# A graph layer and a mixture of experts on one core: masks of the adjacency two pairs sooner in the row products, gathers ahead of additions, seven of eight additions in the neighbour sums

## What is computed

```python
h = layernorm(x)
mask = (adj > 0)                                  # 4096 x 4096, int32 in
agg = mask @ h / max(mask.sum(1), 1)
comb = concat([h @ W_self + b_self, agg @ W_nb + b_nb])
x1 = x + relu(comb @ W_comb + b_comb)
g = layernorm(x1)
score, idx = top_k(g @ Wg + bg, 2)
y = sum over the two experts of softmax(score) * (gelu(g @ W1[e] + b1[e]) @ W2[e] + b2[e])
return x1 + y
```

## Time and profile before

| | us |
|---|---|
| median of 3 runs | 512.1 |
| lowest, highest | 511.46, 516.15 |
| the profiled execution | 515.1 |
| its span, first to last instruction | 513.3 |

### The profile page before, as it was taken

How to read it: one execution, slowest core, us unless ns; L and a number is a source line. 1 busy time by engine, 2 the same in 40 slices (tenths; PEclk the granted TensorE clock), 3 DMA queues, 4 the chain that set the end, 5 groups by cost and what they waited for, 6 DMA issues and landing times.

```text
span 513.3 us, 12757 instructions
## 1 busy us (share of the span) xinstructions
PE 437.3 (85%) x4130; PEld 382.4 (75%) x4130; DVE 391.0 (76%) x1186; ACT 242.9 (47%) x371; POOL 306.7 (60%) x314
## 2 busy tenths in 40 slices
PE   3599969999989969999699699892899999997830
PEld 2489948888878858888588588781689999996610
DVE  2798734578769799798796897877778777779982
ACT  2547545053234424343335243123388888886630
POOL 2569978332335557757576486085768778774570
PEclk9899979999999979999899799995799999999965
DMA  8974999479999999999999994097765565579775
GB/s 247 273 223 129 281 245 263 117 207 262 267 259 258 294 309 277 321 281 307 292 280 298 292 292 155 2 269 250 247 206 175 172 187 173 167 249 407 232 216 164
DMA packets 49168, 122.47 MB, mean 239 GB/s; under 512 B 11081, under 2 KB 20173, under 8 KB 48080
## 3 DMA queue, kind: packets, MB, share of 16 engines
q1 hardware_dynamic: 31632, 68.29, 47.2%
q0 software_dynamic: 16080, 50.49, 32.8%
q10 hardware_dynamic: 1392, 2.88, 1.9%
HBM read 96.52 MB, written 26.93 MB: 240 GB/s over the span
## 4 chain that ended last, share of the span: by engine, by line
DVE 36%; issue 18%; DMA 16%; PE 11%; POOL 9%; ACT 5%; DVEq 3%; SPq 1%; POOLq 0%; ACTq 0%
DMA stage<-in_adj_dram,gidx 12%; DVE rows L1117 5%; PE bank L1229 4%; PE bank L1230 4%; DVE maskT L828 3%; POOL stage L562 3%; ACT mask L670 3%; DMA x_sb<-in_x_dram 2%; POOL rows L586 2%; DVE stage L1123 2%; DVEq L392 2%; DVE w L976 2%; DVE xh L913 2%; ACT w L725 2%; DVE st L923 1%
## 5 line engine op out<-in xcount | busy, mean ns | idle before, releaser
L1229 PE MATMUL bank<-z_flat,maskT 128*128 128x257 f16 x1024 | 232.7, 278 | 0.0
L1230 PE MATMUL bank<-z_lo,maskT 128*128 128x256 f16 x1024 | 232.4, 277 | 0.0
L670 ACT ACTIVATE mask<-stage,m 128x2048 fp8e4<-128x2048 int32 x32 | 64.1, 2003 | 110.1 <-DVE maskT L828 53.4
L562 POOL DMA_INDIRECT stage<-in_adj_dram,gidx x64 | 68.1, 1065 | 74.2 <-ACT mask L670 46.4
L645 POOL DMA_INDIRECT pair_out<-rows,enum x78 | 90.1, 1156 | 37.2 <-issue 20.2
L1229 PEld LDWEIGHTS bank<-z_flat,maskT 128*128 128x128 fp8e4 x1024 | 101.8, 99 | 13.7
L1230 PEld LDWEIGHTS bank<-z_lo,maskT 128*128 128x128 fp8e4 x1024 | 101.7, 99 | 13.0
L573 POOL DMA_INDIRECT dispatched<-rows,slot x64 | 68.1, 1064 | 25.9 <-issue 17.1
L1333 PE MATMUL bank<-stage,w 128*128 128x256 f16 x468 | 59.5, 278 | 4.9 <-DVE stage L1109 4.8
L1353 PE MATMUL bank<-w,stage 128*128 x468 | 59.5, 278 | 2.6 <-DVE stage L1123 2.6
L1238 PE MATMUL bank<-wf,w 128*128 128x256 f16 x384 | 48.3, 287 | 6.6 <-DVE z_lo L883 6.0
(11 more groups left out here) (179 smaller groups left out, 580.9 us busy)
## 6 DMA issues: line engine op xcount, KB each, us to landing
stage<-in_adj_dram SPq DMA_DIRECT2D x256, 128.0 KB
stage<-dispatched SPq DMA_DIRECT2D x39, 260.0 KB, 3.1
wst<-in_L_ffn_W_dram SPq DMA_DIRECT2D x16, 256.0 KB, 10.3
z_lo<-pair_out SPq DMA_DIRECT2D x4, 1024.0 KB, 9.0
dispatched<-pad SPq DMA_DIRECT2D x15, 260.0 KB
out_dram<-x_sb SPq DMA_DIRECT2D x28, 128.0 KB
maskT<-pair_out SPq DMA_DIRECT2D x3, 1024.0 KB, 10.9
x_sb<-in_x_dram ACTq DMA_DIRECT2D x6, 256.0 KB, 10.6
```

Source lines behind the costliest of these rows:

```text
L562: gp.indirect_dma_start(out=stage[:, s, b - 2, :], out_offset=None, in_=adj_q[:, :], in_offset=bass.IndirectOffsetOnAxis(ap=gidx[:, 0:1], ...
L670: sc.activation(mask[:, u % 2, 2:4, :], stage[:, s], ACT.Sigmoid, bias=m100[:, 0:1], scale=200.0, saturate=False).then_inc(s_mA, 1)
L1229: mm(acc[u % 2][:, 0:D + 1], a, z_hi[:, i, :], start=(i == 0), stop=False)
L1230: last = mm(acc[u % 2][:, 0:D], a, z_lo[:, i, :], start=False, stop=(i == NT - 1))
```

## The change

The tables move the six early masks: after pairs 1, 3, 6, 8, 10 and 12 instead of 3, 5, 7, 9, 11 and 13. The statistics of groups 5 to 7 stand ahead of pairs 2, 3 and 5 instead of 1, 2 and 4. On GpSimd gathers 1 to 4 follow the normalisation of groups 2, 4, 5 and 7 instead of 3, 6 and 7 (and, for gather 4, the first addition), gather 5 follows at once, and gathers 6 and 7 stand behind the first addition. The other seven additions go into GpSimd's loop over the sums, in steps 1, 5, 9, ..., 25, between that step's gather and its dispatches. The bias work moves from pairs 1, 3 and 4 to 7, 8 and 9. SP loads the weights of expert 0 behind tile 7 instead of tile 3. No operation is added or left out.

```diff
--- before.py
+++ after.py
@@ -378,8 +378,8 @@
 
 
 
-        MASKS, HELD, MADE = (3, 5, 7, 9, 11, 13), 4, 2
-        STATS = {0: 4, 1: 5, 2: 6, 4: 7}
+        MASKS, HELD, MADE = (1, 3, 6, 8, 10, 12), 4, 2
+        STATS = {0: 4, 2: 5, 3: 6, 5: 7}
 
         def load_experts(eng, held, lags, t, u, known):
 
@@ -454,7 +454,7 @@
                 if t == 0:
                     sp.dma_start(const_bc[:, :], b_comb.rearrange("(o n) -> o n", o=1).to_broadcast((P, D))).then_inc(s_bc, 16)
                     sp.dma_start(bg_bc[:, :], bg.rearrange("(o n) -> o n", o=1).to_broadcast((P, E))).then_inc(s_bc, 16)
-                if t == B - 1:
+                if t == len(MASKS) + 1:
                     load_expert(0)
                 if t >= B + HELD + 1 and t % B == 1:
                     load_expert((t - HELD - 1) // B)
@@ -592,6 +592,7 @@
                 gp.tensor_tensor(rows_f[:, at(B * k, B), 0:D], rows_f[:, at(B * k, B), 0:D],
                                  const_bc[:, :].rearrange("p (o d) -> p o d", o=1).to_broadcast((P, B, D)), ALU.add).then_inc(s_sfc, 1)
 
+
             for k in range(NG):
                 rstd(k)
                 if k == 1:
@@ -600,21 +601,13 @@
                     pool.wait_ge(s_nb, k + 1)
                     for t in range(B * k, B * k + B):
                         normalise(t)
-                if k in (3, 6, 7):
-                    gather((3, 6, 7).index(k) + 1)
+                if k in (2, 4, 5, 7):
+                    gather((2, 4, 5, 7).index(k) + 1)
+            gather(5)
             pool.dma_start(b1c[:, :, :], b1.rearrange("e (t p) -> p e t", p=P), allow_slow_non_contiguous=True).then_inc(s_b12, 16)
             self_and_const(0)
-            gather(4)
-            self_and_const(1)
-            self_and_const(2)
-            gather(5)
-            self_and_const(3)
             gather(6)
-            self_and_const(4)
-            self_and_const(5)
             gather(7)
-            self_and_const(6)
-            self_and_const(7)
 
             LAST_POWERS = NT + X1
             sent = 0
@@ -632,6 +625,8 @@
                     pool.wait_ge(s_lgp, s - PL - 1)
                 if HELD <= s < NT - 2 - MADE:
                     gather(s + 2 + MADE)
+                if s % B == 1 and s // B + 1 < NG:
+                    self_and_const(s // B + 1)
                 for _ in range(1 if s < NT - 2 - MADE else 2):
                     if sent < B * ((s - SLOT + (s == LAST_POWERS - 1)) // B + 1):
                         dispatch(sent)
@@ -889,9 +884,9 @@
                     if 0 < t <= HELD:
                         mask_transpose(t - 1, t - 1, t - 1)
                     masks(t, t, t)
-                if i == 1:
+                if i == 7:
                     biases()
-                if i == 4:
+                if i == 9:
                     const_row()
 
             def main_step(t, u, known):
@@ -1296,7 +1291,7 @@
                     last.then_inc(done, 1)
                 if i + AHEAD < PAIRS:
                     z_transpose(i + AHEAD)
-                if i == 3:
+                if i == 8:
                     const_product()
             pe.wait_ge(s_cst, 6)
             steps(pe, main_step, 3, LAST_RANKS)
```

## The result

The changed kernel is slower: 521.07 us (median of 4 runs, 518.99 to 522.49) against 512.11 us (4 runs, 511.46 to 516.15), a ratio of 1.0173 [1.0128, 1.0218]. The prediction said 506.8 us, in a range up to 513.0.

The account below looks back on a forecast made before the run. The prediction took late gather issue to bound the row products, and VectorE's work and transfers, nearly level, the sums. 515.1 - 7.5 + 2.2 = 509.8, less 3.0 to the median: 506.8 us, range 502.5 to 513.

Parts of the forecast that it names:

- Row products, -7.5 us: Stage before the neighbour sums: earlier masks and gathers remove TensorE's waits, 8.7 us less 0.5 and 0.7, 7.5 us gained.
- its 3.0 us: Profiled execution of the kernel before, 515.1 us, lies 3.0 us above the median of 512.1; taken off the forecast sum.
- Expert 0's weights, "nothing": Weights loaded behind tile 7 on SP, near 75 us, land before step 3 asks near 86 us: no cost.
- Seven additions, +2.2 us: GpSimd additions in the sums hold VectorE; 1.5 us lost for the 32.69 us group and 0.7 for the rest.
- the 7.3 us of slack of five groups: Sums, 150.49 to 321.26 us: each four-step group loses 1.46 us to transfers, waits that could absorb holds of VectorE.
- the bounds: How much of VectorE's holds in the sums reaches the end: between nothing and 9.9 us (7.5, and 2.4 for step 5).
- The additions of steps 1 and 5: Early sums: these additions fall where VectorE still waits for TensorE or a transfer; not among the five holds of 7.5 us.
- The first: Sums: the additions cost nothing, transfer waits absorbing the hold; 504 us, chance 0.20.
- the second: Sums: five holds cost 1.5 us each in full, giving the 7.5 us gain back; 512 us, chance 0.27.
- The third: Sums: all seven additions hold VectorE whole length on the path, 16.5 - 7.5 = +9; 521 us, chance 0.08.

## Why the prediction was wrong

**Row products, -7.5 us: right in the trace, too large in the median.** The sums start at 77.57 where "near 77" was said, no idle time over 1.5 us, a last mask 1.37 us late for "about 1 us", a DMA share of 0.89 for "0.8 or more", gathers 4 at 54.85 and 5 at 59.00 and 60.93 for "53 to 55" and "58 to 60.5". It gave 6.9 us there and 5.0 us between the repeated traces. What the end of the program keeps of it is less: 3.1 us of the median without any addition, so this term was 4.4 us too large. Part of the difference is that the trace of before was taken from a long execution, whose sums started 2.5 us later than in the repeat; I had taken its 3.0 us off the sum but left the gain whole. How the rest is spent was not settled.

**Expert 0's weights, "nothing": right.** The one wait that they caused (1.51 us of VectorE at 88.79) lay in a stretch where TensorE was busy throughout.

**Seven additions, +2.2 us: the step that failed.** The additions cost 9 to 12 us of the medians, not 2.2: of the 14.3 us between forecast and result, this term makes some 9.7 (521.07 - 509.15 - 2.2) and the row products 4.4. Two parts of it were wrong.

*The hold's size and place.* I let the addition start at 248.7, just behind L991 (248.49, 0.17 us long), and hold L998 for 1.5 us. In the changed kernel the subtraction itself is held, for 2.41 us, every time: 12.0 us in five steps where I had 7.5. An instruction that by its recorded 0.17 us would be about over when the addition starts was caught. That it is caught in every step is no chance. The gather ahead of the addition ends 0.15 to 0.17 us after the subtraction's start in all five steps, whether that gather took 1.13 or 1.43 us, and 0.15 to 0.18 us after it in before: 247.61 + 1.04 = 248.65 there, 246.81 + 1.35 = 248.16 here.

*How many holds the waits could absorb.* I set the 7.3 us of slack of five groups against five holds. But only four of the holds lie in these groups. That of step 9 stands ahead of them and came through whole, with another 1.8 us of waiting in the same step; the fifth group has no hold, and its slack is of no use to the others. And I took 2.2 us where the waits were to swallow 5.3 of 7.5, a choice between the bounds that no row gave.

The additions of steps 1 and 5 were rightly counted as free: the second held L910 for 2.47 us, but by step 9 hardly anything of it was left (0.1 us, and 0.4 us in the repeated pair of traces). The way of subtracting the slack comes near in the first pair of traces: the four groups with a hold had lost 135.9 - 4 x 32.69 = 5.1 us before, and 9.6 - 5.1 = 4.5 us stands against 4.9 measured. In the repeated pair it does not: 137.8 us before leaves 9.7 - 7.1 = 2.6 us, and the four groups grew by 5.9. So how much of a hold is absorbed stays open. The losses by place, 515.1 - 6.9 + 4.3 + 5.0 + 1.5 = 519.0, are read from the two traces and so add up to the profiled 518.99 of themselves; they confirm nothing.

**Rivals.** The first (additions cost nothing) fell by the holds, the second (all given back, 512 us) by the size. The third, with a chance of 0.08, gave 521 us and has the mechanism: whole-length holds on the path, TensorE's wait at L1268 up from 15.0 to 21.3 us and the granted clock down from 0.95 to 0.92. Its number is closer than its working, and that is luck: six holds and not seven, about 5 of their 14.5 us absorbed by step 30, and a gain that reached the median with 3 us rather than 7.5. The reason that I gave against it, that the choosing "has instructions before L998 that run on", was where I went wrong.

The Trainium skill ("SBUF — State Buffer", section "SBUF: two separate sides") gives the shared port to whichever of the two instructions starts first, for its whole length, and counts a VectorE instruction with two SBUF inputs only against a GpSimd instruction that reads SBUF. By that rule, the trace agrees for the addition (2.57 to 2.59 us) and for the memset (0.17 us). The same section lets any GpSimd instruction exclude a VectorE instruction in a fast two-port mode; that the memset held the conversion would fit it, but no row tells which mode the conversion ran in. It does not agree on three points: the subtraction has the earlier recorded start, by 0.17 to 0.20 us, and is the one held; the one-input multiplication held it for 1.11 of its 2.82 us, not the whole; and the addition of 0.73 us held it for 0.13 us. Where the two differ, the measurement decides. I had the rule and used it with a starting time of my own; charging the whole length wherever the two overlap would have given 12 us.

## What to carry to other kernels

- Before moving a GpSimd instruction that reads SBUF into a stretch where VectorE is nearly the bound, look up which VectorE instruction stands at the place it will take, and charge its whole length once per occurrence, 0.2 us of misplacement included; then take off only what the same group waits for others now (here 1.46 us on average), and nothing from groups that have no hold.
- Behind the gather of every fourth step the additions cost 9 to 12 us as 128 x 1024. Cut into 128 x 256, one a step, or ahead of the gather, they left the time where it was before. Try the cut or the place before giving up the move.
- A profile of one execution can lie several us above the median. The start of the sums differed by 2.5 us between two traces of the same kernel. A gain read from a wait in one trace should be scaled down before it goes into a forecast of the median.

## What the runs showed of the hardware that was not expected

- The hold depends on the kind and size of the GpSimd instruction that starts 0.15 to 0.25 us behind the same VectorE subtraction: two inputs 128 x 1024 (2.37 us) 2.40 to 2.48 us in 15 of 15 places of three traces; one input 128 x 1024 (2.82 us) 1.11 us and later 0.99 us; memset 128 x 1024 (0.97 us) none, though it held a conversion to its own end; two inputs 128 x 256 (0.73 us) 0.12 to 0.16 us. Why the last is so short was not tested.
- Seven additions in a row (16.22 us from 77.08) held one VectorE instruction from 86.61 to their end (6.99 us). By an even length of 2.32 us for each, an estimate, two of their boundaries lie in this time.
- An addition that starts beside a pair of weight operations holds the pair too: 3.46 us instead of 1.4.
- The gather DMA ahead of the subtraction takes 1.13 to 1.43 us in the change, where most others take 0.93 to 1.06, and ends 0.15 to 0.17 us after the subtraction's start. With the additions ahead of the gather it ended 0.44 to 0.45 us before it in four of five steps, so the tie is not a fixed one. What makes it was not tested.
